# Weighing a group of attention probabilities in one burst of 18 matmuls instead of two parts two units apart

## The reference, cut to what matters

```
xn = layernorm(x, ln_x_g, ln_x_b)            # the 77 context rows
ln = layernorm(latents, ln_l_g, ln_l_b)      # the 1024 tokens
q  = ln @ Wq
kv = concatenate([xn @ Wkv, ln @ Wkv])       # split in k and v, 16 heads of 64
sim  = einsum('bhid,bhjd->bhij', rmsnorm(q, qn_g) * scale, rmsnorm(k, kn_g))
attn = softmax(where(mask, sim, max_neg))
out  = einsum('bhij,bhjd->bhid', attn, v)
return out @ Wout + bout                     # added to the residual
```

## Time and profile before

| what | value |
|---|---|
| median of 3 runs | 2212.14 us |
| the profiled execution | 2211.17 us, its span 2209.4 us |
| PE, matmuls | busy 1952.7 us, 88% of the span |
| DVE | busy 1248.0 us, 56% |
| ACT | busy 1003.0 us, 45% |
| POOL | busy 620.3 us, 28% |
| second attention, units | about 650 to 1829 us of the span |
| L1670, weighing | 2304 PE records, 276.8 us busy |

### The profile page before, as it was taken

One profiled execution on the slowest core, in us unless ns is written; L12 is line 12 of the kernel. 1 busy time (PEld: TensorE's weight loads), 2 busy tenths in 40 slices (PEclk: granted clock), 3 DMA queues, 4 the chain that ended last, 5 costly groups with the idle time before them and its releaser, 6 DMA issues. The chain is left out here.

```text
span 2209.4 us, 40037 instructions
## 1 busy us (share of the span) xinstructions
PE 1952.7 (88%) x13656; PEld 1653.2 (75%) x13657; DVE 1248.0 (56%) x2957; ACT 1003.0 (45%) x1747; POOL 620.3 (28%) x571
## 2 busy tenths in 40 slices
PE   4888947999469999999999999999999984799994
PEld 3477947999257887887788887877778764699994
DVE  5273064676617766776677667667767766122223
ACT  2543314555225555555555555555555541344441
POOL 2300002333164322432343224322432200222220
PEclk9899958999669999999999999999999995899997
DMA  5502163111232113211322123112211207311113
GB/s 195 171 35 79 55 232 108 48 47 45 88 87 51 46 41 69 53 45 41 68 54 48 35 68 68 40 31 68 68 40 30 61 1 269 122 39 37 34 38 126
DMA packets 93663, 159.24 MB, mean 72 GB/s; under 512 B 22385, under 2 KB 54831, under 8 KB 91707
## 3 DMA queue, kind: packets, MB, share of 16 engines
q1 hardware_dynamic: 82875, 134.32, 21.6%
q0 software_dynamic: 8320, 20.65, 3.1%
q10 hardware_dynamic: 2304, 2.10, 0.3%
HBM read 71.57 MB, written 32.41 MB: 47 GB/s over the span
## 5 line engine op out<-in xcount | busy, mean ns | idle before, releaser
L1820 DVE TENSOR_REDUCE a_part_peak<-a_slot 128x1 f32<-128x512 f32 (+1 forms) x512 | 354.4, 731 | 307.7 <-PE a_slot L1645 307.1
L1782 ACT ACTIVATE a_probT<-a_slot 128x640 f32<-128x640 f32 x256 | 180.2, 704 | 475.5 <-PE a_slot L1654 259.5
L1645 PE MATMUL a_slot<-a_KHL,a_QHL 128*128 128x512 f32 (+1 forms) x1536 | 343.6, 359 | 22.1 <-DVE a_probT L1843 11.6
L1645 PEld LDWEIGHTS a_slot<-a_KHL,a_QHL 128*128 128x128 f32 x1536 | 271.8, 190 | 121.6 <-issue 55.1
L1770 ACT ACTIVATE a_prob<-a_slot,a_npeak 128x1024 f32<-128x1024 f32 x256 | 284.0, 1109 | 3.9 <-DVE a_npeak L1822 3.9
L1670 PE MATMUL a_po<-a_probT,a_V 128*64 128x256 f32 (+1 forms) x2304 | 276.8, 384 | 0.0
L1654 PE MATMUL a_slot<-ident,a_prob 128*128 128x128 f32 x2048 | 266.3, 273 | 0.0
L1654 PEld LDWEIGHTS a_slot<-ident,a_prob 128*128 128x128 f32 x2048 | 235.3, 142 | 8.4
L1670 PEld LDWEIGHTS a_po<-a_probT,a_V 128*64 128x64 f32 (+1 forms) x2304 | 153.6, 136 | 87.0 <-issue 21.5
L1597 PE MATMUL a_side<-a_W,a_latT 128*128 128x128 f32 x1536 | 201.1, 282 | 15.9 <-DVE a_KT L1830 10.4
L1597 PEld LDWEIGHTS a_side<-a_W,a_latT 128*128 128x128 f32 x1536 | 187.6, 197 | 21.9 <-DVE a_KT L1830 14.9
(11 more groups left out here) (311 smaller groups left out, 2988.6 us busy)
## 6 DMA issues: line engine op xcount, KB each, us to landing
a_KHL<-a_KT SPq DMA_DIRECT2D x128, 256.0 KB, 4.5
a_QHL<-a_QT SPq DMA_DIRECT2D x128, 128.0 KB, 2.3
m_up<-_L_ffn_gate_up_proj_dram SPq DMA_DIRECT2D x8, 1024.0 KB, 10.4
m_up<-in_L_ffn_W_dram SPq DMA_DIRECT2D x8, 1024.0 KB, 8.6
m_down<-in_L_ffn_W_dram SPq DMA_DIRECT2D x8, 1024.0 KB
a_prob_dram<-a0p_zeros SPq DMA_DIRECT2D x4, 1632.0 KB
a_dist_dram<-a_dist SPq DMA_DIRECT2D x4, 1632.0 KB, 8.1
a_band_prob<-a_prob_dram SPq DMA_DIRECT2D x4, 1632.0 KB, 6.8
```

The source lines that it names most:

```text
L1645: ins = t_.matmul(out[:, lo:hi], q, KHL[:, pair.parity, h, part, lo:hi], start=part == 0, stop=part == 1)
L1782: a_.activation(probT[:, u // 4 % 2, HALF:KT_TILES, h, u % 2 * P:(u % 2 + 1) * P], slot[u % 2][:, HALF * P:KT_TILES * P].rearrange("p (t q ...
L1820: v.tensor_reduce(part[:, i:i + 1], slot[u % 2][:, lo:hi], AX.X, ALU.max).then_inc(part_peaked, 1)
```

## The change

The list PARTS, which says which key blocks `weigh` takes in which part, becomes one part with all nine. PE's loop calls `weigh` once for a group, in units 1, 5, 9 and 13 (`u % 4 == 1`), and no more in units 3, 7, 11 and 15.

```diff
-PARTS = [[8, 0, 1, 2], [3, 4, 5, 6, 7]]
+PARTS = [[8, 0, 1, 2, 3, 4, 5, 6, 7]]
@@ in PE's body, after turn(pair, u) @@
-                    if one_before[0] and u % 2 == 1:
-                        weigh(*one_before, u // 2 % 2)
+                    if one_before[0] and u % 4 == 1:
+                        weigh(*one_before, 0)
```

## The result

| | median us | range | runs |
|---|---|---|---|
| before | 2211.26 | 2209.85 to 2214.71 | 4 |
| changed | 2291.47 | 2288.91 to 2294.48 | 4 |

The ratio is 1.036, 95% interval 1.0343 to 1.0378: 80 us slower. The forecast was 2291 (2266 to 2310). The profiled execution took 2288.91 us, span 2287.0; the two spans differ by 77.6.

A forecast was written before the change was run, and what follows sets the result against it. PE was taken to set the pace; losses of 25.9, 15.0, 21.5, 19.2 and 3.7 us made 85.3, less 5 for the single run: 80 us on 2211.2, so 2291 us, range 2266 to 2310.

The forecast's parts named there:

- The bound: Second attention: PE sets the pace, busy 1139.5 of 1179 us; its busy time stays and the added time is gaps.
- The burst: First odd units: one run of matmuls saves 0.08 us a group, at most 0.15; 63 x 0.08 = 5 us gained.
- The burst's wait: Burst in unit 5 waiting for the group before to be normalised: cost put at nothing.
- Unit 15: Pairs 0 to 14: next turn waits for ACT's exponentials; 1.31 us back, 1.00 lost, 15 times, 15.0 us.
- Unit 7: Pairs 0 to 14: reductions wait for DVE's spread; 0.88 us back, 1.43 lost, 15 times, 21.5 us.
- Unit 3: Pairs 1 to 14: DVE's spread, slow beside POOL, holds the next scores; 0.46 us back, 1.85 lost, 25.9 us.
- Unit 11: Pairs 0 to 14: spread delays reductions and L1830 behind them; 1.03 us back, 1.28 lost, 15 times, 19.2 us.
- Pairs: Second attention: the stage grows by 80 us, some 5.5 us a pair.
- Pair 0 and pair 15: Pair 0 has no unit 3 move; pair 15, without POOL, loses 0.93 us four times, 3.7 us.
- Only the copies count: Rival, units 3, 7 and 11: DVE's lateness does not reach PE, taking away 18.2 us: 2273 us; chance 0.24.
- The clock falls: Rival: new PE gaps put a tenth of its time at 1.2 GHz, adding 114 us: 2405 us; chance 0.04.
- The lock: DVE's spread at unit 3 is blocked by POOL on a shared port, 1.29 us, and does not shrink when PE comes sooner.

The follow-up runs named there:

- the filler: Changed kernel plus 60 sets of 6 unused identity transposes in units 3, 7, 11 and 15: 2285.65 us, ratio to before 1.0346.
- the written-out kernels: Loops over pairs written out without jumps: kernel before 2197.15 us, changed kernel 2267.79, kernel before with last pair weighed in three parts 2192.33.
- the run with the spread on ACT: Changed kernel with the inverse sums spread by ScalarE in place of VectorE: 2277.82 us, ratio to before 1.0294.
- 12 + 6: Kernel before with parts of 12 and 6 matmuls in place of 8 and 10, so 4 move: 2219.45 us, ratio 1.0024.

## Why the prediction was right, point by point

The gaps stand where the forecast had them and end by what it named. But the agreement of 2291 with 2291.47 is in part luck: the gaps came out about 8 us cheaper than their terms, and the clock, at nothing in the sum, made up most of it.

- **The bound.** Right. PE set the pace, and most of the cost is gaps: the filler went in for nothing, and the cost bends with what stays. But PE's busy time did not stay. Over the stage it is 13.1 us more (1124.37 to 1137.49) beside 65 us more of idle time. Part of this is the clock; the written-out kernels, at 1.00, still have 9.4 us more, which no run takes apart (PE's ends are modelled).
- **The burst.** I took 0.08 of a possible 0.15 us saved by the single run; all of it came, +2.16 and not 2.23. That is 0.28 us a pair too dear.
- **The burst's wait** for the group before, put at nothing: right, PE has 0.0 us of idle time ahead of L1670.
- **Unit 15.** 1.31 back forecast, 1.31 measured.
- **Unit 7.** 0.88 forecast, 0.86 measured.
- **Unit 3.** 0.46 forecast, 0.61 measured. The mechanism is shown by the run with the spread on ACT. Of the 0.15 missing, 0.11 is seen in the rows: DVE's reductions start 1.21 after the spread's start, where before it was 1.32. I put this to DVE's instructions overlapping more when they are queued; no run tests it.
- **Unit 11.** 1.03 forecast, 1.16 measured, I think by the same overlap.
- **Pairs.** So a middle pair costs 4.70, where my terms gave 5.56 - 0.32 = 5.24: 7.5 us too much over 14 pairs. This is the mis-sized part of the sum.
- **Pair 0 and pair 15.** My terms gave 3.5 and 3.4. Written out, with the clock at 1.00 in both kernels, they cost 3.3, and 4.7 less the 1.5 that unit 15 gives back behind the last L1652, so 3.2. In the kernels with loops pair 0 shows only 2.2, since its first unit in the kernel before still ran at half clock (0.50 until 660.3 us, 5.91 us long and not 4.86), and unit 15 gives back only 0.2, since the clock fell there after the change.
- **The jumps.** Not in the sum. PE's wait there grew from 4.6 to 9.9 us, but it takes the place of a wait for DVE that the kernel before had, and costs nearly nothing in sum (above).
- **Only the copies count** (2273): fell. The lock term is there, but with 12 us, less than the 18 I gave it.
- **The clock falls** (2405): fell with its 114 us, but the forecast put the clock at nothing, and it costs: about 6 us in unit 0 of pairs 3, 11 and 13, and 1.2 behind the last L1652, less the 1 us of half clock in pair 0 of the kernel before. So without it the change would cost some 72 us in place of 78, and the forecast of 80 would have been 8 too high; the written-out kernels say 70.5 (72.0 - 1.5). Windows on these stretches, behind three of the four jumps and at pair 15's end:

```profile
886.30:893.70 7.40, 7.40 (x46) 6.89 (x48) 3.47 (x9) 2.77 (x6) 0.00 (x0) 0.77 0.01 3
1510.00:1515.00 5.00, 5.00 (x29) 4.87 (x29) 1.27 (x5) 2.53 (x5) 0.00 (x0) 0.66 0.02 5
1667.90:1674.80 6.90, 6.08 (x27) 5.99 (x28) 1.24 (x4) 2.45 (x5) 0.00 (x0) 0.51 0.02 5
1893.00:1902.80 9.80, 8.95 (x51) 5.81 (x51) 2.98 (x9) 0.70 (x1) 0.00 (x0) 0.65 0.01 2
```

  There the clock was at 1.2 GHz in place of 2.4 for a part of the stretch, with the fall during or right behind an idle stretch of PE, of 2.54 to 2.59 us at a jump and of 2.20 at the end. After the 2.25 us in pair 5 it did not fall. Nor does the idle time alone tell: in the kernel before the same wait of 2.20 us stands at the end, and the clock over the 10 us from it is 1.00:

```profile
1815.23 0.70 PE L1687 MATMUL a_slot<-a1o_Wout,a_OT 128*128 128x256 f32 x2 [2.20 <-ACT a_prob L1771]
1815.00:1825.00 10.00, 9.55 (x73) 6.02 (x73) 3.06 (x9) 0.88 (x2) 0.00 (x0) 1.00 0.01 2
```

  The gaps of 0.79 to 1.22 us alone never did this: the window of pair 15 above is at 1.00, and the changed kernel written out has no such stretch. The rule of the Trainium skill on small idles between groups of matmuls (TensorE: Matmul & The Clock Gate, "A second HAM failure mode: psum-queue depth-cycling"), which the page tells of a bf16 kernel, is so not borne out here for float32 matmuls and gaps of about 1 us.
- **The lock** (the Trainium skill, SBUF — State Buffer, "Who interferes with whom": of VectorE in a 2-port mode and GpSimd, whichever comes first holds the shared port pair for its whole instruction, and the other waits). In which mode the spread runs no run shows. The trace agrees in the lengths: 1.29 us beside POOL before and after, 0.29 without, and on ACT 0.41 to 0.42 in all 64, with POOL busy or not. It agrees in when the spread is let go too. In both kernels 45 of the 64 spreads start while an instruction of POOL runs, and each of them ends 0.14 to 0.16 us after the end of that instruction; the other 19 take 0.29 or 0.30. Unit 11 of pair 5 after the change, where POOL ends at 1103.43 and the spread at 1103.57:

```profile
1102.14 1.29 POOL L1575 TENSOR_TENSOR a_QT<-a_qgam,a_QT 128x512 fp32r<-128x512 f32 x1
1102.41 1.16 DVE L1862 COPY a_rwide<-a_rsum 128x256 f32<-128x256 f32 x1
```

## What to carry to other kernels

Work that fills a wait has a size to meet: here 0.8 to 1.2 us behind each unit, and six matmuls did nearly all of it where ten stood. Ask of each piece of work on the bounding engine which wait it covers before gathering it; the total does not tell. Behind a full unit there can be a queue of another engine (here a copy held up by GpSimd) that costs nothing until the cover goes. And a total that agrees is not yet a sum that agrees: here the clock behind the loops' jumps hid that the gaps had been priced too high.

## What the runs showed of the hardware that I had not expected

- At a jump of its loop TensorE stood idle longer after the change, where its scores had waited, than before, where matmuls ran ahead of them: 3.58 us from the scores to the next turn against 2.16. VectorE stood idle 2.91 us at its own jump in both.
- Writing the loops out made the kernel before 0.6% faster (ratio 0.9938), and no long stall is seen in the attention. One unit each in pairs 1, 3 and 4 is 0.19 to 0.24 us longer than in the other pairs, the same units in all three written-out kernels; whether the longer code does this is open.
- The clock of the changed kernel's second attention fell at four of its five idle stretches of 2.2 to 2.6 us and in no stretch with gaps of about 1 us. In other runs it fell behind 1.83 us (12 + 6) and stayed behind 2.31 (the useless work), so the length of the idle stretch alone does not tell.
- A copy of VectorE that starts while GpSimd's instruction runs ends 0.14 to 0.16 us after that instruction does, 45 times of 45.
